# One GpSimd add per key tile instead of two, and a new calendar, in a cross-attention and mixture-attention kernel

## The reference

```python
x = x + _L0_xattn_ref(_layernorm(x), ctx, ctx, lens, Wq, Wk, Wv, Wo)     # 16 heads of 32, keys masked past lens
hidden = _layernorm(x)
pooled = hidden.mean(axis=1)                                             # per batch
logits = relu(pooled @ gw1.T + gb1) @ gw2.T + gb2                        # 8 experts
top_vals, top_idx = top_k(logits, 2); gates = softmax(top_vals)
# each of q, k, v, o:  hidden @ Wm.T + sum over 2 experts of gates * (hidden @ V.T * S) @ U.T + b
attn = softmax(einsum('bhsd,bhtd->bhst', q, k))                          # 16 heads of 32, 512 x 512 each
x = x + out_projection(einsum('bhst,bhtd->bhsd', attn, v))
```

## Time and profile before

| what | value |
|---|---|
| time, median of 3 runs | 1611.27 us (1607.5 to 1613.24) |
| the profiled execution: its own time | 1609.4 us |
| its span in the profile | 1607.6 us |
| granted TensorE clock, mean over the span | 0.955 |
| TensorE (PE) busy | 1483.9 us (92%), 5752 matmuls |
| VectorE (DVE) busy | 975.2 us (61%) |
| ScalarE (ACT) busy | 792.4 us (49%) |
| GpSimd (POOL) busy | 614.2 us (38%), of which 452 us in 192 adds of probabilities |
| DMA queue of SyncE | 132.81 MB, 30.7% of 16 engines |

### The profile page before, as it was taken

The page is one execution under the profiler, slowest core; times in us unless marked ns, Lnnn a source line. Parts: engine busy times, 40 slices in busy tenths (PEclk is TensorE's granted clock), DMA queues, the critical chain, the costliest instruction groups (busy, mean ns, idle before and its releaser), DMA issues.

```text
span 1607.6 us, 17017 instructions
## 1 busy us (share of the span) xinstructions
PE 1483.9 (92%) x5752; PEld 724.3 (45%) x5752; DVE 975.2 (61%) x1732; ACT 792.4 (49%) x1362; POOL 614.2 (38%) x381
## 2 busy tenths in 40 slices
PE   6566799999999999989999999989998999999987
PEld 3332344445454454444444545445444545444432
DVE  2223545675677657775677567765677567766553
ACT  0222155465555655475555555464546555454451
POOL 3000101353444533263344534362325344454474
PEclk9766799899999999999999999999999999999998
DMA  6313122432323421532334322423253232232220
GB/s 216 76 45 101 60 69 51 122 93 67 80 61 118 99 80 45 135 93 70 77 84 138 85 67 47 132 79 93 50 145 96 66 77 58 79 99 72 53 54 27
DMA packets 78573, 134.95 MB, mean 84 GB/s; under 512 B 22854, under 2 KB 25542, under 8 KB 75415
## 3 DMA queue, kind: packets, MB, share of 16 engines
q1 hardware_dynamic: 74391, 132.81, 30.7%
q10 hardware_dynamic: 4096, 1.06, 0.3%
HBM read 70.22 MB, written 12.21 MB: 51 GB/s over the span
## 4 chain that ended last, share of the span: by engine, by line
PE 80%; DMA 5%; ACT 5%; SPq 4%; DVE 3%; issue 2%; ACTq 1%; POOL 0%; DVEq 0%; POOLq 0%
PE pj L978 38%; PE sc L1031 8%; PE scT L1059 7%; PE pj L1007 6%; PE acc L1088 6%; PE sc L1020 4%; DMA ks<-ks 3%; PE scT L1052 2%; PE pj L1076 2%; PE pj L1068 2%; SPq L510 2%; PE pj L972 2%; PE pj L1097 1%; SPq L459 1%; PE pj L964 1%
## 5 line engine op out<-in xcount | busy, mean ns | idle before, releaser
L717 ACT ACTIVATE probs<-scT 128x512 f32<-128x512 f32 x512 | 289.8, 595 | 409.3 <-PE scT L1059 405.4
L821 DVE TENSOR_REDUCE negmax<-sc 128x1 f32<-128x512 f32 x512 | 338.8, 680 | 168.2 <-PE sc L1031 165.1
L607 POOL TENSOR_TENSOR probs_sum<-probs_sum,probs 128x1024 f32<-128x1024 f32 x128 | 300.6, 2360 | 101.8 <-ACT probs L717 101.8
L1031 PE MATMUL sc<-ks,qs 96*128 96x512 f32 x512 | 277.9, 569 | 19.4 <-DMA ks<-ks 18.1
L603 POOL TENSOR_TENSOR probs_sum<-probs 128x1024 f32<-128x1024 f32 x64 | 151.4, 2371 | 364.8 <-ACT probs L717 198.2
L847 DVE RECIPROCAL inv_sum<-pj 128x128 f32<-128x128 f32 x256 | 226.9, 923 | 73.8 <-PE pj L1097 42.8
L1059 PE MATMUL scT<-qs,ks 99*128 99x512 f32 x512 | 264.4, 550 | 6.4 <-ACT probs L717 3.2
L978 PE MATMUL pj<-XT,Wqk 128*128 128x512 f32 x512 | 256.5, 602 | 0.0
L578 POOL TENSOR_TENSOR xhat<-xhat,inv_sum 128x128 f32<-128x128 f32 (+1 forms) x56 | 45.1, 806 | 377.2 <-DVE inv_sum L847 377.2
L1031 PEld LDWEIGHTS sc<-ks,qs 96*128 96x128 f32 x512 | 96.0, 191 | 132.2 <-issue 89.0
L1007 PE MATMUL pj<-U_sb,V_sb 128*128 128x512 f32 x256 | 134.6, 621 | 16.8 <-ACT V_sb L629 15.9
(11 more groups left out here) (93 smaller groups left out, 1629.3 us busy)
## 6 DMA issues: line engine op xcount, KB each, us to landing
Wvo<-in_WmT SPq DMA_DIRECT2D x16, 1024.0 KB, 6.9
Wqk<-in_WmT SPq DMA_DIRECT2D x16, 1024.0 KB, 6.3
X<-in_x SPq DMA_DIRECT2D x8, 1024.0 KB, 7.1
qsc<-stage_lo SPq DMA_DIRECT2D x128, 64.0 KB, 2.0
qsc<-qsc SPq DMA_DIRECT2D x32, 256.0 KB, 3.0
U_sb<-in_U SPq DMA_DIRECT2D x32, 256.0 KB, 4.1
V_sb<-in_V SPq DMA_DIRECT2D x32, 256.0 KB, 4.6
qs<-stage_lo SPq DMA_DIRECT2D x128, 64.0 KB, 2.0
```

The source lines that it names most:

```text
L607: nc.gpsimd.tensor_tensor(probs_sum[:, pair], probs_sum[:, pair], probs[:, kt % 2, pair], ALU.add)\
L717: nc.scalar.activation(probs[:, kt % 2, jj, :], scT[:, ST[step], :], ACT.Exp, scale=SCALE)\
L821: nc.vector.tensor_reduce(negmax[:, 0, n:n + 1], sc[:, SC[step], :], AX.X, ALU.max, negate=True)\
L1031: nc.tensor.matmul(sc[:, SC[step], :], qs[0:3 * DH, slot, jj, t * P:(t + 1) * P], ks[0:3 * DH, slot, jj, :], start=True, stop=True).then_i ...
```

## The change

`psum` loses its index h (the pair of heads). One instruction adds all four heads of a key tile: 128x2048 elements in place of two times 128x1024, 96 instructions in place of 192. It waits for the exponential of the fourth head, where the first pair waited for the second head's. ScalarE waits before the first head of a key tile for the whole earlier add, where it waited before heads 0 and 2 for that pair's add. `den` waits for the one add of key tile 3. And the calendar is another one: nearly every number differs, and with it the order on all engines.

```diff
-           "psum": product(JOBS, range(1, TT), PAIR), "accout": product(JOBS), "den": product(JOBS),
+           "psum": product(JOBS, range(1, TT)), "accout": product(JOBS), "den": product(JOBS),
...
-    "wm_load": (-99, 12, -271, 2739),
+    "wm_load": (-105, 0, -8, 2702),
...
-            def psum(step, b, j, kt, h):
-                pair = slice(2 * h, 2 * h + 2)
-                pool.wait_ge("exp_done", pool.after("exp_done", "sT", b, j, kt, 2 * h + 1))
+            def psum(step, b, j, kt):
+                pool.wait_ge("exp_done", pool.after("exp_done", "sT", b, j, kt, HJ - 1))
                 if kt == 1:
...
-                    nc.gpsimd.tensor_tensor(probs_sum[:, pair], probs[:, 0, pair], probs[:, 1, pair], ALU.add)\
+                    nc.gpsimd.tensor_tensor(probs_sum[:], probs[:, 0], probs[:, 1], ALU.add)\
                         .then_inc(sems["probs_added"], 1)
                 else:
-                    pool.wait_ge("probs_added", pool.after("probs_added", "psum", b, j, kt - 1, h))
-                    nc.gpsimd.tensor_tensor(probs_sum[:, pair], probs_sum[:, pair], probs[:, kt % 2, pair], ALU.add)\
+                    pool.wait_ge("probs_added", pool.after("probs_added", "psum", b, j, kt - 1))
+                    nc.gpsimd.tensor_tensor(probs_sum[:], probs_sum[:], probs[:, kt % 2], ALU.add)\
                         .then_inc(sems["probs_added"], 1)
...
                 if jj == 0:
                     act.wait_ge("pv_done", act.after("pv_done", "pv", *before))
-                if jj % 2 == 0:
                     added = (b, j, kt - 1) if kt == 2 else before
-                    act.wait_ge("probs_added", act.after("probs_added", "psum", *added, jj // 2))
+                    act.wait_ge("probs_added", act.after("probs_added", "psum", *added))
...
-                pe.wait_ge("probs_added", pe.after("probs_added", "psum", b, j, TT - 1, 1))
+                pe.wait_ge("probs_added", pe.after("probs_added", "psum", b, j, TT - 1))
```

More of the change, by code:

```diff
@@ L53 @@
[L53 to L61, removed]
@@ L71 @@
[L71 to L77, removed]
@@ L96 @@
-    "divide": (2097, 2306, 2929, 3066, 3084, 3114, 3139),
-    "out2": (3102, 3123, 3136, 3140, 3172, 3183, 3190, 3235, 3296, 3328, 3328, 3371, 3434, 3447, 3453, 3472),
-    "residual2": (3168, 3344, 3409, 3484),
+    "context": (-1809,),
+    "load": (-2339,),
+    "stats": (-2257, -2254, -2165, -2113),
+    "deviation": (-2076, -282),
+    "normalize": (-1990, -260),
+    "xpose": (-1947, -1933, -1927, -1883, -202, -201, -177, -165),
+    "q1": (-1862, -1858, -1836, -1833, -1542, -1538, -1519, -1511, -1270, -1251, -1203, -1202, -1178, -1161, -1153,
+        -1142),
@@ new lines @@
+    "q1_split": (-1802, -1463, -1177, -1081),
+    "q1_rows": (-1790, -1390, -1139, -911),
+    "q1_stack": (-1780, -1318, -1127, -902),
+    "uv_load": (-1409, -603, 154, 2659),
+    "csc": (-1664, -1634, -1609, -1592, -1314, -1299, -1296, -1292, -1056, -1056, -1049, -1047, -761, -751, -744,
+        -721),
+    "cross_shift": (-1543, -1273, -1029, -714),
+    "cross_shift_move": (-1520, -1261, -1023, -691),
+    "csT": (-1462, -1440, -1430, -1414, -1200, -1195, -1175, -1173, -962, -937, -917, -915, -668, -660, -611, -610),
@@ new lines @@
+    "cpv": (-1330, -1144, -869, -588),
+    "cacc": (-1301, -1133, -864, -583),
+    "cden": (-1275, -987, -872, -594),
+    "cinv": (-1249, -1242, -1226, -1207, -962, -956, -915, -914, -852, -840, -798, -771, -562, -551, -545, -475),
+    "wm_load": (-105, 0, -8, 2702),
+    "cdivide": (-1116, -910, -717, -559, -490, -448, -433),
+    "out1": (-637, -609, -546, -507, -536, -481, -470, -442, -442, -422, -419, -380, -360, -358, -346, -337),
+    "residual1": (-505, -420, -364, -309),
+    "residual_bias": (2059,),
@@ new lines @@
+    "token_sums": (-191, -168, -168, -150),
+    "gate_hidden": (-79,),
+    "gate_top": (-71,),
+    "scale_v": (-49, -19, 179, 2761),
+    "weff": (-21, -18, -4, -3, 41, 79, 81, 245, 273, 282, 319, 347, 2837, 2899, 3015, 3061),
+    "qk": (13, 14, 88, 130, 191, 215, 258, 297, 647, 664, 671, 692, 717, 719, 734, 736, 904, 904, 909, 941, 1222,
+        1236, 1262, 1289, 1719, 1793, 1854, 1886, 1895, 1930, 1962, 1978),
+    "qk_split": (205, 307, 704, 754, 1001, 1338, 1900, 1985),
+    "qk_rows": (335, 384, 762, 815, 1294, 1362, 1982, 1998),
@@ new lines @@
+    "qk_stack": (427, 520, 818, 873, 1305, 1369, 2045, 2077),
+    "v": (324, 337, 353, 439, 362, 405, 445, 480, 539, 549, 568, 605, 597, 626, 643, 645),
+    "v_bias": (444, 509, 612, 699),
[4 rows of a table added]
+    "shift": (874, 1358, 1899, 2409),
+    "shift_move": (909, 1413, 1958, 2456),
[5 rows of a table added]
+    "psum": (1102, 1262, 1266, 1666, 1863, 1959, 2131, 2369, 2531, 2625, 2734, 2772),
+    "accout": (1690, 2052, 2562, 2942),
+    "den": (1354, 1990, 2558, 2919),
+    "inv": (1367, 1371, 1379, 1418, 2052, 2064, 2070, 2098, 2566, 2613, 2617, 2643, 2922, 2929, 2945, 2946),
@@ L99 @@
+    "divide": (1852, 2914, 2725, 2990, 3025, 3110, 3111),
+    "out2": (2979, 3031, 3040, 3093, 3147, 3159, 3159, 3218, 3333, 3353, 3354, 3367, 3369, 3378, 3409, 3429),
+    "residual2": (3133, 3314, 3384, 3454),
 }
 OWN = {
[L105 to L108, removed]
@@ L109 @@
[L109 to L113 removed]
[4 rows of a table removed]
+    "context_keys": {(0, 0): -3491, (0, 1): -3097, (1, 0): -2604, (1, 1): -2590, (2, 0): -2483, (2, 1): -2426,
+        (3, 0): -2243, (3, 1): -2108},
+    "split_keys": {(): -2010},
+    "context_values": {(0,): -6305, (1,): -5674, (2,): -5105, (3,): -4920, (4,): -4476},
+    "context": {(0,): -1687},
@@ L118 @@
+    "wm_load": {(7, 3): 16507},
+    "uv_load": {(7, 3): 15854},
+    "scale_v": {(7, 3): 23982},
+    "weff": {(7, 3, 0): 27301, (7, 3, 1): 28276, (7, 3, 2): 29419, (7, 3, 3): 30671},
[4 rows of a table added]
 }
```

32 lines of the change are left out of this document (removed), and 26 rows, old and new, of tables (CALENDAR, OWN).

## The result

The changed kernel takes 1626.5 us (median of 4 runs, 1624.1 to 1627.2); the kernel before, 1609.4 us in its 4 (1595.2 to 1613.2). The ratio is 1.0105, 95% interval [1.0059, 1.0152]: slower by 1%, at the forecast 1626. The profiled execution has a span of 1625.4 us at a mean clock of 0.942, against 1607.6 and 0.955. TensorE's busy time went from 1483.9 to 1494.0 us (same matmuls, so that is the clock and overlap), its idle time from 123.7 to 131.4. More than half of the 17.8 us is thus not idle time at all.

The account below looks back on a forecast made before the run. TensorE, busy 172.21 of 177.4 us per steady batch, was taken as the bound, so only its idle time could move. Terms 23.8 - 13.8 + 5.7 + 1.5 = +17.2 on 1609.4 gave 1626 us, range 1602 to 1634.

Parts of the forecast that it names:

- the likeliest case: The forecast's own case, all terms as summed: 1617 to 1634 us by its bounds, chance 0.46.
- The adds themselves, 0: Mid-batch, ScalarE's longer wait for an add is covered by TensorE's work; batch 0's +1.3 us is given back: zero together.
- The gate, +23.8: At seven gates `hiddenB` waits out a longer add: TensorE idle 5.45 us instead of 2.05 each, +23.8 us together.
- idle 1.35: From `gate_top` to `weff`, 5.85 us with 4.5 us of matmuls in it, so TensorE idles 1.35 us.
- The rival in which the clock falls: Longer gate waits drop the clock twice at each of seven gates; about 12 us on top, 1638 us; chance 0.12.
- The stacked keys, -13.8: At the gates of batches 1 to 6, TensorE's wait for job 3's stacked keys' copy goes: -13.8 us.
- in SyncE's new order that transfer stands ahead: The 1 MB `Wqk` transfer goes ahead of the queries' stacking, some 6 us earlier, and is over before the keys' copy.
- The first batch, +5.7: Batch 0's cross-attention loses time in three stages, +1.5, +2.0 and +2.2: +5.7 us, between 3 and 8.
- The first piece, +1.5: First batch: all eight matmuls now stand right before `csT`, where six did: +1.5 us.
- The last piece: First batch, last stage: two `out1` steps leave the wait for the shift and stand in the full part behind: +2.2 us.
- they are one chain: First batch: `csT`, its exponentials, row copies, their DMA and the next `csc` form one chain, so added matmuls delay it.
- The end, +1.5: Last job: adds take 16.2 us instead of 13.9, starting about 0.8 us earlier: +1.5 us, between 0 and 4.

Follow-up runs that it names:

- e9: Changed kernel with 4 idle matmuls ahead of TensorE's wait for `hiddenB` in batches 1 to 7: 1619.4 us, 1.0054 of the kernel before.
- e1: Changed kernel's new calendar, with two 1024-column adds per key tile in place of each 2048-column one: 0.9963 of the kernel before.
- e12: Changed kernel with the 1 MB keys' matrix fetched where it was before, between stacking job 3's queries and keys: 1633.1 us, 1.0151 of the kernel before.
- e8: Changed kernel with the first batch's cross-attention in the old order (121 steps): 1634.9 us, 1.0144 of the kernel before.
- e7: Changed kernel, whole adds, with the last batch from job 1's projections on in the old order: 1637.5 us, 1.0167 of the kernel before.
- e10: e1 (adds in pairs) with the last batch from job 1's projections on in the old order: 1605.0 us, 0.9956 of the kernel before.
- e6: Changed kernel with `hiddenB` computed on ScalarE right behind the ReLU instead of on VectorE: 1616.5 us, 1.0046 of the kernel before.
- e11: e10 with `hiddenB` computed on ScalarE: 1602.0 us, 0.9955 of the kernel before.

## Why the prediction was right, and where its terms were not

The total came out to the microsecond, and that is largely luck. Laid on the stretches of the table above, the terms are 5.7 + 3.6 = +9.3 (the first batch and the wait for `hiddenB` at the first of the seven gates), +6.6, -0.2 - 0.8 = -1.0 (what remains of the last gate, and the earlier start of the adds) and +2.3; measured are -2.3, +9.3, +8.2 and +2.7. So the first came out 11.6 us below the forecast and the third 9.2 above it. Also, the likeliest case by its own bounds spans 1619 to 1635, not 1617 to 1634.

**The adds themselves, 0: right.** In the steady batches ScalarE never waits for an add. It does so twice in the last batch, 9.6 us together; the one at 1589.19 keeps TensorE waiting for 4.56 us and belongs to the end, the other costs TensorE nothing.

**The gate, +23.8: right, in another shape.** The block is as described: the first add ends 0.6 us before `hiddenB` wants to start (I had 0.35), `hiddenB` takes 3.95 us (4.3), `gate_top` waits 3.46 (4.1), the cast is free (0.17). The step that failed is "idle 1.35" before `weff`: I had its matmuls at full speed. The clock fell behind the 3.46 us of standstill and stretched them over the wait for `V_sb`. Against e9 the slower clock costs 174.9 - 173.1 = 1.8 us of busy time a batch on average, so a gate costs 3.46 + 1.8 - 2.05 = +3.2 us where I had +3.4. The rival in which the clock falls had the mechanism right, at all seven gates, though with twice 3.4 us at three of them only. Its 12 us were spent (7 x 1.8 = 12.6), but "on top" is wrong: they stand in the place of the wait that I had counted. e1 shows the whole thing from the other side, 23 us for the length of the add alone.

**The stacked keys, -13.8: right in size, its cause half shown.** All six waits went. TensorE reaches the first `sc` of job 3 as long behind the first `weff` as before (711.07 - 701.98 = 9.1 us; before 711.22 - 3.14 - 698.76 = 9.3), and the copy is issued 4.5 us behind `weff` instead of 5.0; so it is mainly the copy that is shorter, 3.2 us instead of 7.31. That the 1 MB in flight makes it long fits: with the transfer put back (e12) it takes 4.8 us on average instead of 3.8. But that is 1.0 of the 2.5 us by which it is shorter than before, and only 0.8 us of waiting returns. So the step "in SyncE's new order that transfer stands ahead" names a part of the cause. The rest comes with something else in the new kernel; the two are further apart at some gates, but at the gate of batch 2 they are not, and what it is stays open. The place in the queue was worth about 3 us by the trace; by the medians, whose intervals overlap, up to 7.

**The first batch, +5.7: wrong.** The first `weff` stands at 192.11, not at 198, 0.5 us earlier than before. TensorE of the changed kernel, beside the earlier trace rows:

```profile
95.42 0.94 PE L1049 MATMUL scT<-qsc,keys 99*77 99x512 f32 x2 [0.70 <-ACT probs L704]
105.48 3.64 PE L1017 MATMUL sc<-keys,qsc 97*128 97x78 f32 x16 [7.29 <-DMA qsc<-qsc]
126.82 3.42 PE L1017 MATMUL sc<-keys,qsc 97*128 97x78 f32 x15 [5.35 <-DMA qsc<-qsc]
157.28 1.14 PE L1049 MATMUL scT<-qsc,keys 99*77 99x512 f32 x2 [6.55 <-DMA qsc<-shift]
```

The first piece, +1.5, is there at the first `csT` (95.42 for 93.96). One stage later it is gone: the third `csc` starts at 126.82 where it started at 126.85. The last piece is there too (157.28 for 155.72) and is gone at the next transposes. The failed step is "they are one chain": I added work to a part that was full, and did not ask what the same move takes out of the next part, where the second stage lost two short waits. Why the last stage gives its 1.6 us back I can't say from these runs; e8 shows no more than that the new order of this part is not the slower one. Between the first `weff` and the gate of batch 1 another 5.0 us of TensorE's busy time went, at a higher clock, for which I had no term.

**The end, +1.5: the chain right, the stretch before it not.** From the first add of job 3 to the end it is +2.7 us; GpSimd and TensorE of the changed kernel show the chain that I had added up, 16.7 us where I had 16.2:

```profile
1584.32 4.50 POOL L601 TENSOR_TENSOR probs_sum<-probs 128x2048 f32<-128x2048 f32 x1 [5.27 <-DVE inv_sum L844]
1591.83 9.20 POOL L605 TENSOR_TENSOR probs_sum<-probs_sum,probs 128x2048 f32<-128x2048 f32 x2 [1.78 <-ACT probs L714]
...
1601.18 1.77 PE L1094 MATMUL pj<-probs_sum,ones 128*32 128x512 f32 x8 [2.46 <-POOL probs_sum L605]
```

But 8.2 us more are lost between the last `gate_top` and that first add, a stretch for which I had -1.0 (the last wait for `hiddenB` lies ahead of it). Of the 8.2, TensorE's busy time has 7.7, in 569 matmul records instead of 562, and its idle time 0.5; the clock there is 0.90 instead of 0.95. The largest part is one spell: from 1561 to 1577 the granted clock is 0.50 throughout, behind waits of 1.79 us for the stacked keys and 0.55 us for a row maximum, with TensorE busy for 15.1 of the 16 us. The kernel before has a spell of 7 us there, behind a wait of 2.90 us at 1562.8; the 10 us more, at half speed, are worth about 5 us by this estimate. I had no term for the clock at the end. That neither order nor pairs bring it back (e1, e7, e10: 214.0, 225.0, 215.7) says that the cause is not the one thing I tried; why the spell is so long stays open.

**The steady part** altogether: 6 x 3.4 - 13.8 = +6.6 forecast, +9.3 measured. With a gate at +3.2 the terms give +5.4, so some 4 us are in neither. Most of them are TensorE's busy time: at full clock a batch has 172.3 us before (the first four stretches) and 173.1 in e9 without the filling, for the same matmuls in another order.

## What to carry to other kernels

Before two short instructions of GpSimd are merged into a long one, look for the small VectorE instructions in a chain that TensorE waits for: one that reads two inputs from SBUF, or a tensor_scalar or cast from SBUF to SBUF, can wait out the whole of the long one, and here that was worth 1.4% in a kernel whose GpSimd is idle for 60% of the time. Put such an instruction on another engine only after looking for what ends next; here much of the gain went to the next waits (e6), or all of it (e11). A standstill of TensorE is to be priced with the clock behind it, and where work stands right behind it, the next wait in line is then partly paid already. And a total that comes out right proves no term: lay the terms on the stretches of the trace; two of the four here were off by 9 us and more.
